# Selective scans of an audio tower: where the parts of y are added up, on TensorE or on GpSimd

## What is computed

```
dbc = x @ W_dbc.T;  delta, B, C = split(dbc)          # 1, 64, 64
delta = softplus(delta * W_dt + b_dt)                 # one value per token and feature
h_t[e, n] = exp(delta_t[e] * A[e, n]) * h_{t-1}[e, n] + delta_t[e] * x_t[e] * B_t[n]
y_t[e]    = sum_n h_t[e, n] * C_t[n]  +  D[e] * x_t[e]
x_next    = mean of y over pairs of tokens            # after layers 1 and 2
```

## Time and profile before

| | us |
|---|---|
| median of three runs | 811.09 |
| the profiled execution: its time | 812.87 |
| its span, first to last instruction | 810.7 |
| busy in the span: TensorE | 721.1 (89%) |
| VectorE | 548.2 (68%) |
| ScalarE | 425.1 (52%) |
| GpSimd | 439.2 (54%) |

### The profile page before, as it was taken

One profiled execution on the slowest core, in us unless ns is written; L12 is line 12 of the kernel. 1 busy time (PEld: TensorE's weight loads), 2 busy tenths in 40 slices (PEclk: granted clock), 3 DMA queues, 4 the chain that ended last, 5 costly groups with the idle time before them and its releaser, 6 DMA issues.

```text
span 810.7 us, 11084 instructions
## 1 busy us (share of the span) xinstructions
PE 721.1 (89%) x3474; PEld 360.3 (44%) x3474; DVE 548.2 (68%) x859; ACT 425.1 (52%) x761; POOL 439.2 (54%) x402
## 2 busy tenths in 40 slices
PE   4789898989899894858999988879999999999997
PEld 2344444545444452326767767733333333333332
DVE  3389899989989897574578888556445445444543
ACT  1778676868786875433445554333433433433432
POOL 1458768686878675845565555243344444434440
PEclk9699999999999997778999999989999999999999
DMA  4446565435344552142000000190954444334400
GB/s 127 137 124 155 125 154 135 120 85 129 92 118 119 129 143 58 39 96 49 1 2 3 4 3 4 29 181 4 197 120 94 102 102 102 86 87 82 108 1 19
DMA packets 30097, 70.20 MB, mean 87 GB/s; under 512 B 4483, under 2 KB 20175, under 8 KB 29647
## 3 DMA queue, kind: packets, MB, share of 16 engines
q1 hardware_dynamic: 29727, 68.77, 35.7%
q10 hardware_dynamic: 304, 0.63, 0.2%
HBM read 66.96 MB, written 2.43 MB: 86 GB/s over the span
## 4 chain that ended last, share of the span: by engine, by line
PE 45%; DVE 8%; ACT 2%; issue 1%; DVEq 0%; ACTq 0%
PE pair L863 22%; PE pair L884 11%; PE pair L766 4%; PE pair L798 3%; PE pair L749 3%; PE pair L785 1%; PE pair L813 1%; DVE big L1489 1%; PE pair L807 1%; ACT big L1153 1%; DVE big L1494 1%; DVE big L1543 0%; DVE big L1554 0%; DVE big L1553 0%; DVE big L1564 0%
## 5 line engine op out<-in xcount | busy, mean ns | idle before, releaser
L1652 DVE TENSOR_TENSOR hidden<-pair,tmp 128x502 f32<-128x502 f32 (+1 forms) x192 | 121.6, 675 | 130.2 <-PE pair L863 105.7
L1778 POOL TENSOR_TENSOR hidden<-xs,big 128x502 f32<-128x502 f32 (+1 forms) x96 | 111.8, 1166 | 169.5 <-PE pair L863 146.9
L1210 ACT ACTIVATE tmp<-pair 128x502 f32<-128x502 f32 (+1 forms) x192 | 102.5, 586 | 157.1 <-PE pair L863 157.1
L1804 POOL TENSOR_TENSOR big<-big 94x512 f32<-94x512 f32 (+3 forms) x120 | 89.1, 775 | 68.0 <-DVE big L1553 58.8
L863 PE MATMUL pair<-xs,w 64*128 64x502 f32 (+1 forms) x384 | 108.1, 640 | 0.5 <-DVE big L1585 0.5
L863 PE MATMUL pair<-hidden,w 64*128 64x502 f32 (+1 forms) x384 | 98.5, 589 | 1.8 <-DVE hidden L1652 1.8
L1350 DVE TENSOR_TENSOR_SCAN pair<-tmp,pair 128x750 f32<-128x750 f32 (+1 forms) x56 | 96.0, 1713 | 0.4
L884 PE MATMUL pair<-hidden,w 128*64 128x502 f32 (+1 forms) x384 | 91.1, 596 | 0.0
L1674 POOL TENSOR_TENSOR big<-big,work 128x750 f32<-128x750 f32 (+1 forms) x28 | 45.6, 1628 | 50.8 <-ACT big L941 50.8
L484 PE MATMUL pair<-big,work 128*128 128x512 f32 x112 | 61.4, 630 | 4.1 <-DVE work L1362 4.1
L863 PEld LDWEIGHTS pair<-xs,w 64*128 64x128 f32 x384 | 29.7, 187 | 67.3 <-issue 36.4
(11 more groups left out here) (185 smaller groups left out, 1268.6 us busy)
## 6 DMA issues: line engine op xcount, KB each, us to landing
big<-dispatched SPq DMA_DIRECT2D x40, 502.0 KB, 6.7
spread<-rowsd SPq DMA_DIRECT2D x48, 375.0 KB, 5.7
spread<-rowsd SPq DMA_DIRECT2D x48, 187.5 KB, 3.4
big<-in_x SPq DMA_DIRECT2D x12, 375.0 KB, 6.1
big<-dispatched SPq DMA_DIRECT2D x8, 498.0 KB, 5.8
spread<-rowsd SPq DMA_DIRECT2D x8, 374.0 KB, 4.9
w<-in_w SPq DMA_DIRECT2D x5, 512.0 KB, 6.8
big<-in_x SPq DMA_DIRECT2D x1, 1500.0 KB, 7.0
```

The lines of the kernel that those rows point to most:

```text
L1210: act.activation(sT[i % 4][:, 0:w], bank[BANK1[i]][:, 0:w], ACT.Silu).then_inc(silu_a, 1)
L1652: v.tensor_tensor(hidT[i % 8][:, 0:hi - lo], bank[BANK2[i]][:, 0:hi - lo], sT[i % 4][:, 0:hi - lo], ALU.mult)\
L1778: pool.tensor_tensor(xw[e % 4][:, 0:hi - lo], xs[:, lo:hi], wx[:, e, 0:hi - lo], ALU.mult)\
L1804: ins = eng.tensor_tensor(dst[:, :, at:at + H * m].rearrange("p u (h d) -> p u h d", d=m), t[:, :, :, 0:m], t[:, :, :, k:D], ALU.mult)
```

## The change

For the units of layers 1 and 2:

- `by_delta` isn't run. `output` writes y0T = pairs[3] * u, without D.
- `sums` part 0 begins with four more matmuls: a diagonal matrix of D / 2 (`diag`, built in the setup by VectorE in place of the halving of D) times the even and the odd tokens of x, and the identity times those of y0T. It waits for `y_v` between the two. The accumulation in `bank[1]` now holds all of y.
- GpSimd's `add` does nothing. ScalarE's copy completes the unit.

Units of layer 3 are computed as before. Waits follow: `made(eng, n)` is ScalarE's copy (`sm_a`) for layers 1 and 2 and `xa_g` for layer 3; `used(eng, n)`, that the buffers of unit n are free, is `pl_p`, TensorE's last matmul of `sums`. The counts of `t_v`, `yp_g` and `xa_g` start with layer 3.

```diff
+        def used(eng, n):
+            if TAKES[n]:
+                eng.wait_ge(pl_p, TAKEN[n])
+            else:
+                eng.wait_ge(xa_g, n - LAST_LAYER + 1)
+
+        def made(eng, n):
+            if TAKES[n]:
+                eng.wait_ge(sm_a, TAKEN[n])
+            else:
+                eng.wait_ge(xa_g, n - LAST_LAYER + 1)
...
             def sums(n, part):
-                _, l, _, _ = unit(n)
+                _, l, _, x = unit(n)
                 if l == 2:
                     return
                 if part == 0:
                     after(pe, sm_a, TAKEN[n] - 1)
+                    for k, t in enumerate(halves(x, l)):
+                        pe.matmul(parts(bank[1], l), diag[:, l, :], t, start=(k == 0), stop=False)
+                    pe.wait_ge(y_v, n + 1)
+                    for t in halves(y0T[n % 3], l):
+                        pe.matmul(parts(bank[1], l), ident, t, start=False, stop=False)
                 pe.wait_ge(hc_v, STATIC * n + part + 1)
                 for k, t in enumerate(halves(hC[n % 2][part], l)):
-                    mm = pe.matmul(parts(bank[1], l), ident, t, start=(part == 0 and k == 0),
-                                   stop=(part == 1 and k == 1))
+                    mm = pe.matmul(parts(bank[1], l), ident, t, start=False, stop=(part == 1 and k == 1))
...
-                v.tensor_scalar(dskip[:, 0:2], dskip[:, 0:2], 0.5, None, ALU.mult)
+                for l in range(2):
+                    v.tensor_scalar(diag[:, l, :], ident, dskip[:, l:l + 1], 0.5, ALU.mult, ALU.mult)
...
             def by_delta(n):
-                _, _, w, _ = unit(n)
+                _, l, w, _ = unit(n)
+                if l < 2:
+                    return
...
             def output(n):
                 _, l, w, x = unit(n)
-                v.wait_ge(t_v, n + 1)
-                after(v, xa_g, n - 2)
+                if n > 2:
+                    used(v, n - 3)
+                if l < 2:
+                    v.wait_ge(s_p, n + 1)
+                    v.wait_ge(u_g, n + 1)
+                    v.tensor_tensor(y0T[n % 3][:, 0:w], pairs[3][:, 0:w], of(u, n), ALU.mult).then_inc(y_v, 1)
+                    return
+                v.wait_ge(t_v, n - LAST_LAYER + 1)
...
             def add(n):
-                _, l, _, _ = unit(n)
-                pool.wait_ge(y_v, n + 1)
-                if l < 2:
-                    even, odd = halves(y0T[n % 3], l)
-                    after(pool, xa_g, n)
-                    pool.tensor_tensor(parts(pT, l), even, odd, ALU.add).then_inc(yp_g, 1)
-                    pool.wait_ge(yp_g, n + 1)
-                    pool.wait_ge(sm_a, TAKEN[n])
-                    pool.tensor_tensor(pooled(n), pooled(n), parts(pT, l), ALU.add).then_inc(xa_g, 1)
-                else:
-                    first_part(n)
+                if TAKES[n]:
+                    return
+                first_part(n)
...
```

More of the change, by code:

```diff
@@ L69 @@
 LAST = UB[NP - 1]
+LAST_LAYER = UB[6]
 Z_OF = UNITS
@@ L126, in program @@
         averaging = sb("averaging", [128, 128])
+        diag = sb("diag", [128, 2, 128])
         eps = sb("eps", [128, 1])
@@ L433, in _ @@
                     sp.dma_start(dst, src).then_inc(later_in, 16)
-            sp.wait_ge(xa_g, UNITS)
+            made(sp, UNITS - 1)
             sp.wait_ge(more_g, MG[NP])
@@ L490, in x_ready @@
                     src_p, src_n = source(p, n)
-                    pe.wait_ge(xa_g, src_n + 1)
+                    made(pe, src_n)
                     pe.wait_ge(more_g, MG[src_p + 1])
@@ L669, in period @@
                     pe.wait_ge(rw_a, len(EVENTS))
-                    pe.wait_ge(xa_g, LAST)
+                    made(pe, LAST - 1)
                     pe.wait_ge(more_g, MG[NP - 1])
@@ L817, in attention @@
             def attention():
-                pe.wait_ge(xa_g, UNITS)
+                made(pe, UNITS - 1)
                 pe.wait_ge(more_g, MG[NP])
@@ L1168, in attention @@
             def attention():
-                act.wait_ge(xa_g, UNITS)
+                made(act, UNITS - 1)
                 act.wait_ge(more_g, MG[NP])
@@ L1355, in read @@
                 v.wait_ge(sc_v, STATIC * n + j + 1)
[L1356 to L1359, removed]
+                if n > 1:
+                    used(v, n - 2)
                 if j == 1 and n == UB[p] + 1 and p:
@@ L1367, in last_add @@
                 n = UNITS - 1
-                v.wait_ge(yp_g, n + 1)
+                v.wait_ge(yp_g, n - LAST_LAYER + 1)
                 v.wait_ge(hc_v, STATIC * (n + 1))
@@ L1377, in more_slots @@
                 with v.If(m > STATIC):
-                    v.wait_ge(xa_g, last + 1)
+                    used(v, last)
                     with v.Fori(0, MORE) as i:
@@ L1692, in add @@
             def add(n):
-                _, l, _, _ = unit(n)
-                pool.wait_ge(y_v, n + 1)
-                if l < 2:
-                    even, odd = halves(y0T[n % 3], l)
-                    after(pool, xa_g, n)
-                    pool.tensor_tensor(parts(pT, l), even, odd, ALU.add).then_inc(yp_g, 1)
-                    pool.wait_ge(yp_g, n + 1)
-                    pool.wait_ge(sm_a, TAKEN[n])
-                    pool.tensor_tensor(pooled(n), pooled(n), parts(pT, l), ALU.add).then_inc(xa_g, 1)
-                else:
-                    first_part(n)
-                    pool.wait_ge(yp_g, n + 1)
-                    pool.wait_ge(hc_v, STATIC * (n + 1))
-                    pool.tensor_tensor(pooled(n), pooled(n), seqs(hC[n % 2][1], 2), ALU.add).then_inc(xa_g, 1)
+                if TAKES[n]:
+                    return
+                first_part(n)
+                pool.wait_ge(yp_g, n - LAST_LAYER + 1)
+                pool.wait_ge(hc_v, STATIC * (n + 1))
+                pool.tensor_tensor(pooled(n), pooled(n), seqs(hC[n % 2][1], 2), ALU.add).then_inc(xa_g, 1)
             def more_slots(p):
@@ L1713, in more_slots @@
                 with pool.If(m > STATIC):
-                    pool.wait_ge(xa_g, last + 1)
+                    made(pool, last)
                     with pool.Fori(0, MORE) as i:
@@ L1757, in attention @@
             def attention():
-                pool.wait_ge(xa_g, UNITS)
+                made(pool, UNITS - 1)
                 pool.wait_ge(more_g, MG[NP])
```

## The result

The changed kernel took 856.1 us in the median of four runs (852.7 to 859.1), the kernel before beside it 810.6 (809.99 to 812.42). The ratio is 1.056 with a 95% interval of 1.050 to 1.061: 5.6% slower. The profiled execution took 858.67 us with a span of 855.9, 45.2 us over that of before. Predicted were 856.0 us in a range of 846 to 867.

What follows compares the result with a forecast made beforehand. TensorE and VectorE both stood at 90% in the scans; TensorE's queue was to set the pace. 63.4 us of new matmuls less 18.45 us of closed gaps gave +44.95, so 811.09 became 856.0 us, range 846 to 867.

Steps and rivals of the forecast that it cites:

- The price of two matmuls: TensorE, `sums` part 0: two new matmuls cost 1.32 us, four 2.64, over 24 units 63.4 us added.
- VectorE's 23.7 us: VectorE, scans of layers 1 and 2: 0.99 us less busy time in each of 24 units, 23.7 us.
- the 3 to 4 that I gave as a sign: Sign in the changed profile: VectorE idles 3 to 4 us a unit before `load` or `product`, waiting for TensorE.
- The gaps before `mixed` and `weighted_b`: TensorE's waits for VectorE's `output` and `read` close: 8.8 and 4.1 us back, plus 2.4 us of covered tails.
- The maximum: TensorE's six waits for VectorE's maximum in the scans: 2.7 us come back, 7.4 of 10.1 stay.
- Unit 0: First unit: VectorE, without `by_delta`, is 0.95 us earlier for `mixed` (0.91 us wait), scan and reduction 1.7 us earlier.
- The clock variant: TensorE from 47.3 to 52 us: full clock returns, 1.7 us less, 854.3; a third of the cases inside the forecast.
- GpSimd's last add, 0.45 us: End of layer 2's scans: no final add to wait for, `extreme_rows` up to 1.9 us earlier, 0.45 us back.
- Layer 3 and all behind it unchanged: Phases of layer 3, attention and experts: same instructions, only shifted, length unchanged.
- No gap closes: Rival, scans: TensorE's idle time moves with it as a chain, all +63.4 us is added, 874.5 us; 6%.
- the price is off: Rival, `sums`: the new group doesn't stream, each record costs 0.49 us, +76 us, 887 us; 3%.
- VectorE stays the bound: Rival, `mixed` and `weighted_b`: new matmuls fit TensorE's slack, VectorE's 23.7 us come off, 787 us; 3%.

Runs made afterwards that it cites:

- e11: The changed kernel run again, with its own trace: 853.66 us in six runs, ratio 1.052 to the kernel before.
- e1: Kernel before plus four matmuls per unit in `sums` part 0 that multiply zeros, VectorE's and GpSimd's old work kept: 857.35 us, ratio 1.057.
- e2: Kernel before without `by_delta` in layers 1 and 2 and with the change's `output`, D x left out: 800.76 us, ratio 0.989.
- e3: Changed kernel without the identity matmuls on y0T, which GpSimd adds as before; the diagonal on x stays: 823.61 us, ratio 1.015 to the kernel before.
- e4: Changed kernel without the diagonal matmuls on x; `by_delta` and old `output` stay, identity on y0T kept: 826.58 us, ratio 1.019 to the kernel before.
- e6: Changed kernel with y0T, D x / 2 and hC in bf16, all eight matmuls of the sums: 782.28 us, ratio 0.965 to the kernel before.
- e10: Changed kernel with y0T and hC in bf16, GpSimd adding x's even and odd tokens for one fp32 D x matmul: 786.27 us, ratio 0.965.
- e8: Changed kernel plus three unread matmuls in TensorE's idle time of unit 0, before `extreme_rows`: 852.75 us, ratio 1.051 to the kernel before.
- e5: Changed kernel with the four new matmuls in bf16 (y0T, and D x / 2 made by GpSimd): 810.3 us, ratio 0.998 to the kernel before.
- e7: VectorE's part of the change alone, with D x computed by GpSimd and ScalarE, against the kernel before: 824.95 us, ratio 1.016.

## Why the prediction was right, point by point

- *The number.* 856.0 forecast, 856.1 measured; a second set of the same program has its median at 853.66 (e11), so the match to 0.1 us is luck, and so are parts of the sum, as shown below.
- *Which engine sets the pace.* Right, and shown by e1 and e2 apart: TensorE's part alone gives the whole loss, VectorE's alone a gain of 10 us.
- *The price of two matmuls, 1.32 us.* Right to 0.01 us in the trace of after, and again as the step from e3 or e4 to the whole change, 29.5 and 32.5 us against 31.7 (27 and 30 with the median of e11).
- *VectorE's 23.7 us.* Somewhat too much. Its busy time is 224.9 us from 31 to 352 us, but 226.7 to 354.5, where the scans end, against 248.9 before: 22.2 less, and 20.2 by the page's totals. I had priced it by the recorded lengths of 0.94 us, while VectorE's operations in a row start 0.84 us apart (in the trace of before at 40.04, 40.88 and 41.72). It became idle time. In front of `load` and `product` it is 2.4 us a unit (31.2 and 25.8 by 24), not the 3 to 4 that I gave as a sign.
- *The gaps before `mixed` and `weighted_b`, 12.9 us and their tails.* Closed, as said. e1 closes them without VectorE, all but the first 0.9 us, which I had rightly given to it.
- *The maximum: 2.7 of 10.1 us back.* It gave 1.4 (8.7 stay, 7.4 were forecast). The first of the six waits did shrink, from 2.89 to 1.16 us, but what had been won there went elsewhere, see the next point. The other five should have shrunk by 0.2 each and did not: 7.2 us before, 7.5 after, where the one of the earlier trace rows went from 1.55 to 1.35 and others grew. Why is open.
- *Unit 0.* This step failed. VectorE was earlier as said, `mixed` of unit 1 starts at 35.83 us instead of 37.59 (0.7 us of that is luck: the 512 columns of `summed` in front, at 33.18 us in both traces, took 1.12 us instead of 1.85, at the higher clock). Then VectorE ran into a wait that the trace of before had just covered, the DMA of the C rows. VectorE and TensorE of the changed kernel in order of time:

```profile
...
42.40 0.94 DVE L1391 TENSOR_TENSOR tmp<-pair,spread 128x750 f32<-128x750 f32 x1 [1.94 <-DMA spread<-rowsd]
```

```profile
...
43.39 2.73 PE L523 MATMUL pair<-big,w0pm 128*32 128x375 f32 x16 [2.20 <-DVE tmp L1391]
47.28 0.59 PE L585 MATMUL pair<-packed,smx 128*1 128x128 f32 x2 [1.16 <-DVE smx L1306]
47.79 2.08 PE L501 MATMUL pair<-big,work 128*128 128x512 f32 x2
...
54.86 0.51 PE L538 MATMUL pair<-big,rowsel 128*32 128x375 f32 x2
```

`read` at 42.40 had waited 1.94 us for its rows; before, it began at 41.72 without a wait. The issues of these rows, before and then after, with that `read` of before:

```profile
...
35.94 1.09 SPq L406 DMA_DIRECT2D spread<-rowsd  x2
...
41.72 0.93 DVE L1362 TENSOR_TENSOR tmp<-pair,spread 128x750 f32<-128x750 f32 x1
```

```profile
...
35.85 1.09 SPq L423 DMA_DIRECT2D spread<-rowsd  x2
```

From the issue to `read` it is 5.8 us before (the rows may have landed earlier) and 6.55 after. So about 1.2 us of the wait were there to be run into, and some 0.75 are a slower transfer in this execution; e6 and e10, with the same `by_delta` gone, have 5.8 and 6.0 us. TensorE idled 2.20 us before `extreme_rows` and then ran at the lower of its two levels: 2.73 us for what took 1.47 in the earlier trace rows, and 2.08 instead of 1.18 in `weighted_b`. The next unit's rows came at 54.86 us, against 53.54 before. I had 2.6 us of gain there (0.9 for `mixed`, 1.7 for the maximum) and it is 1.3 us of loss. I had named it as a sign of being wrong that TensorE waits for something that didn't delay it before, and for this step that is what came. The clock variant, which I gave a third, went the other way: the granted clock of the stretch is 0.54, lower than before. What my estimate lacked was that the idle time would move, not go. The Trainium skill (TensorE: Matmul & The Clock Gate, The HAM clock gate) ties the clock to how busy TensorE has lately been. The filling of e8, with a granted clock of 1.00, agrees with that.
- *GpSimd's last add, 0.45 us.* `extreme_rows` at the end of layer 2 came 45.9 us later than before, the reduction behind it 47.0 later, so 1.2 of the 1.9 us were lost again, as said (1.45).
- *Layer 3 and all behind it unchanged.* Not quite: from the reduction at the end of layer 2 (310.03 us before, 357.07 after) to the end it is 500.7 us before and 498.8 after. Most of it is one wait in the decision of layer 3's weights, TensorE for ScalarE. Total, times, longest, first before, then after:

```profile
...
PE pair L573 <- ACT amax L973: 5.9, 1, 5.9
```

```profile
...
PE pair L594 <- ACT amax L994: 3.5, 1, 3.5
```

I have no experiment on it, so its cause stays open. The 45.2 us of the two spans thus came out at the forecast 45.0 by misses that cancel. In the scans to that reduction it is 47.0 us, 2.1 more than forecast: unit 0 was 3.9 worse (2.6 of gain that became 1.3 of loss), the rest of the scans some 1.8 better, although the maximum gave less there. Behind the scans it is 1.8 less. Where the rest of the scans won is not traced.
- *The rivals.* "No gap closes" would have been 874; "the price is off" 887; "VectorE stays the bound" is the state that e6 reaches, with the new and the old sums at a quarter of the price. The slack that I gave this rival was too large: I had all 23.7 us won up to 0.64 us of new matmuls a unit and nothing lost up to about 1.6, but e5 comes out only even at 0.67 (with one more operation of GpSimd), and e2 without any new ones wins 10.

## What to carry to other kernels

Where two engines stand at 90%, add up one queue: the work moved onto it at its start-to-start price, less the gaps that it can fill; what the other engine is spared counts only as far as it closes gaps of the first that the longer queue would leave open. Before sums are moved onto TensorE, look at the type: in fp32 two matmuls of 375 columns took 1.32 us, in bf16 0.33, and that decides: with all four new ones in fp32 the kernel is 5.6% slower, in bf16 even, and with the four old ones in bf16 too 3.5% faster (at lower precision). A mean share of busy time is no room on an in-order engine, as GpSimd showed in e7: look at what stands behind the wait.

## What the runs showed that I had not expected

- Added work made a stretch faster in the trace: with 2 us of idle matmuls in unit 0 the next unit's rows came 4.0 us earlier, while TensorE stayed at its upper clock level (granted clock 1.00 instead of 0.54 from 43 to 54 us).
- One and the same program spreads by 1% (851.1 to 860.8 us in six runs of the changed kernel), which hides effects of 3 us even in sets of six.
- A bf16 identity matmul of 375 columns streams at 0.165 to 0.17 us behind and ahead of fp32 ones, without a gap at the change of type (e5).
